# A linear-attention stage in four pipeline stages with row tiles of two heads, and softmax probabilities scaled before their transposes

## The reference, cut to what matters

```python
# block 1: linear attention, 16 heads of 16 features, chunks (64 in the reference; the kernel uses 128)
q = (q @ fq1.T + b) * (q @ fq2.T + b);  k = (k @ fk1.T + b) * (k @ fk2.T + b)
s = where(tril, qc @ kc.T, 0);  o = s @ vc + qc @ state;  state += kc.T @ vc
o = o * rsqrt(mean(o*o) + eps) * norm_w;  x = x + layernorm(o @ wo.T)
# block 2: softmax attention, 32 query heads in 8 groups of 4, head size 64, causal
attn = softmax(where(causal, q @ k.T / 8, min));  h = r + (attn @ v) @ wo
# then a mixture of 8 experts (top 2), then x = x + layernorm(h + moe)
```

## Time and profile before

| | us |
|---|---|
| median of three runs | 1934.72 |
| the profiled execution, its own time | 1933.22 |
| its span, first to last instruction | 1931.3 |
| PE busy in it | 1813.6 |
| DVE busy in it | 1055.0 |
| ACT busy in it | 924.1 |

### The profile page before, as it was taken

How to read it: one execution, slowest core, us unless ns; L and a number is a source line. 1 busy time by engine, 2 the same in 40 slices (tenths; PEclk the granted TensorE clock), 3 DMA queues, 4 the chain that set the end, 5 groups by cost and what they waited for, 6 DMA issues and landing times.

```text
span 1931.3 us, 32217 instructions
## 1 busy us (share of the span) xinstructions
PE 1813.6 (94%) x12286; PEld 1428.7 (74%) x12286; DVE 1055.0 (55%) x2465; ACT 924.1 (48%) x2049; POOL 261.1 (14%) x355
## 2 busy tenths in 40 slices
PE   6999689999999999999999999999985999999994
PEld 5666457777777777777777777777765999999993
DVE  3666556766776766767767667667655111111112
ACT  3343255655656656656656656656651222222223
POOL 2222110000000000000000000000001222222222
PEclk9999889999999999999999999999986999999997
DMA  2000010000000000000000000000017134213443
GB/s 83 0 0 0 0 44 1 9 1 1 9 1 1 9 1 1 10 1 1 9 1 1 9 1 1 1 1 1 23 34 245 22 92 128 48 26 87 119 125 95
DMA packets 46042, 60.02 MB, mean 31 GB/s; under 512 B 8944, under 2 KB 39536, under 8 KB 45936
## 3 DMA queue, kind: packets, MB, share of 16 engines
q1 hardware_dynamic: 36336, 46.16, 7.2%
q0 software_dynamic: 7536, 10.36, 3.2%
q10 hardware_dynamic: 2064, 2.10, 0.3%
HBM read 138.43 MB, written 11.40 MB: 78 GB/s over the span
## 4 chain that ended last, share of the span: by engine, by line
PE 86%; DVE 7%; ACT 2%; issue 2%; POOL 1%; DMA 1%; SPq 0%; DVEq 0%; POOLq 0%; ACTq 0%
PE wide L1401 15%; PE bank L1313 13%; PE bank L1301 12%; PE bank L1253 9%; PE wide L1285 8%; PE bank L1410 7%; PE wide L1286 7%; PE bank L1322 6%; PE wide L1120 2%; PE bank L1109 2%; PE bank L1298 1%; ACT qhl L634 1%; PE bank L1177 1%; DVE arena L802 1%; PE bank L1243 1%
## 5 line engine op out<-in xcount | busy, mean ns | idle before, releaser
L884 DVE CUSTOM_DVE_ANT_0 arena<-wide,arena 128x896 f32<-128x896 f32 (+7 forms) x512 | 383.8, 755 | 223.2 <-PE wide L1286 219.3
L640 ACT ACTIVATE arena<-arena,nmax 128x896 f32<-128x896 f32 (+7 forms) x512 | 397.0, 776 | 177.3 <-DVE nmax L884 174.2
L1285 PE MATMUL wide<-khi,qhl 128*128 128x512 f32 (+3 forms) x768 | 346.3, 452 | 1.7 <-DVE qhl L877 1.7
L1301 PE MATMUL bank<-ident,arena 128*128 128x128 f32 x2304 | 308.5, 274 | 0.0
L648 ACT COPY arena<-bank 128x512 f32<-128x512 f32 (+1 forms) x352 | 191.7, 545 | 214.0 <-PE bank L1301 206.3
L1401 PEld LDWEIGHTS wide<-wo,arena 128*128 128x128 f32 x2496 | 287.0, 193 | 3.2 <-issue 1.3
L1401 PE MATMUL wide<-wo,arena 128*128 128x128 f32 x2496 | 287.3, 277 | 0.9 <-ACT wo L693 0.9
L1313 PE MATMUL bank<-arena,vt 128*64 128x256 f32 x2304 | 277.0, 385 | 0.0
L1301 PEld LDWEIGHTS bank<-ident,arena 128*128 128x128 f32 x2304 | 262.3, 141 | 16.6 <-issue 0.4
L1286 PE MATMUL wide<-klo,qhl 128*128 128x512 f32 (+3 forms) x768 | 256.0, 347 | 0.0
L1050 DVE TENSOR_TENSOR wo<-wide,wo 128x512 f32<-128x512 f32 x78 | 53.9, 692 | 368.1 <-PE wide L1401 368.1
(11 more groups left out here) (221 smaller groups left out, 1749.8 us busy)
## 6 DMA issues: line engine op xcount, KB each, us to landing
arena<-in_L_ffn_w SPq DMA_DIRECT2D x117, 1024.0 KB
x_all<-in_L_attn_x ACTq DMA_DIRECT2D x1, 2048.0 KB, 9.9
wq_g<-in_L_ffn_wq SPq DMA_DIRECT2D x8, 256.0 KB, 3.5
wo<-in_L_ffn_wo SPq DMA_DIRECT2D x16, 128.0 KB, 3.0
hbuf<-acc SPq DMA_DIRECT2D x2, 1024.0 KB, 4.6
tbuf<-rT_all SPq DMA_DIRECT2D x4, 512.0 KB, 3.0
acc<-hbuf SPq DMA_DIRECT2D x4, 512.0 KB, 5.5
out<-x_all SPq DMA_DIRECT2D x8, 256.0 KB, 2.1
```

The lines of the kernel that those rows point to most:

```text
L640: nc.scalar.activation(probs[t % 2][:, h, 0:w], probs[t % 2][:, h, 0:w], ACT.Exp, bias=nmax[:, t % 2, h:h + 1], scale=-1.0, accum_out=rsum ...
L884: nc.vector.tensor_tensor_reduce(out=probs[t % 2][:, h, 0:w], in0=score_bank(t, h)[:, 0:w], in1=causal[:, SEQ - w:SEQ], scale=-1.0, scalar ...
L1285: mm(dst, q, khi[:, lo:lo + cols], start=True, stop=False)
L1301: ins = nc.tensor.transpose(to[:, h * P:(h + 1) * P], probs[t % 2][:, h, m * P:(m + 1) * P], ident[:])
```

## The change: what it does

In the linear-attention stage all loops are unrolled, and a tile goes through four steps where it went through two: front in step s, output in step s+1, layer norms in step s+2, last transpose in step s+3 (so there are 11 steps, of which 8 have a front). `qx` keeps two masked copies per half, with a mask that leaves one head of each 32 rows (`rowmask`); a score call is now 8 matmuls of 32 rows by 256 columns each, four row groups writing to four banks. There are two score calls per step, of 8 matmuls each. Masks 2 and 3 of a tile move to the next step. x is normalised by ScalarE (a new `xnmr`), the state add and the first residual add move from VectorE to GpSimd, and ScalarE copies the output projection to SBUF (`aos`).

In the softmax stage the spread block of `rinv` is gone from GpSimd and TensorE. VectorE multiplies each head's probabilities in place by the inverse row sum (`normalise`) and transposes wait for that. All block evacuations and the copy of the weighted values (`oT`) are ScalarE's.

```diff
-NCONST = 27
+NCONST = 29
+ROWS = 4
+HR = HB // ROWS
-    blocks = t % TB + 2
+    blocks = t % TB + 1
...
 # GpSimd, linear attention
-                    for b in range(BATCH):
-                        nc.gpsimd.tensor_tensor(qx[:, 0, b], qT[:, 0, b:b + 1, :].to_broadcast([P, HB, P]), ...
+                if back:
+                    power(s - 2, BATCH, rstds["ao"], ves["ao"], "ve_ao", "rstd_ao")
+                    gp.wait_ge(S("aon_ready"), s - 1)
+                    nc.gpsimd.tensor_tensor(xb, xb, aon, ALU.add).then_inc(S("x1_ready"), 1)
+                if mid and s < TB:
+                    nc.gpsimd.tensor_tensor(state, state, kvt, ALU.add).then_inc(S("state_ready"), 1)
+                if front:
+                    nc.gpsimd.tensor_tensor(qx[:, 0].rearrange("p b h c -> p h b c"), ... [P, HR, BATCH, P]), ALU.mult)
...
 # ScalarE, linear attention
-                    for h in range(HB):
-                        ins = nc.scalar.activation(qx[:, 1, :, h], qT[:, 1], ACT.Copy, scale=headmask[:, h:h + 1])
+                    for h in range(HR):
+                        ins = nc.scalar.activation(qx[:, 1, :, h], qT[:, 1], ACT.Copy, scale=rowmask[:, h:h + 1])
+                    nc.scalar.copy(aos, bank[0][:].rearrange("p (b d) -> p b d", b=BATCH)).then_inc(S("aos_ready"), 1)
+                if s + 1 < TB:
+                    normal_x(s + 1)
...
 # VectorE, linear attention: the order of a step
+                if mid:
+                    mask(s - 1, 2)
+                    mask(s - 1, 3)
+                if back:       # layer norm of aos, tile s-2
+                    variance(i, aos, "ao")
...            # q, then variance of x1, both reciprocals, k, onT, y
+                if front:
+                    mask(s, 0)
+                    mask(s, 1)
...
 # TensorE, linear attention
-                    for j in range(2):
-                        ins = mm(wide[:, 2 * b + j, :], kT[:, k, b], qx[:, k, b, j * 4:(j + 1) * 4]...)
+                def score(k):
+                    if s or k:
+                        pe.wait_ge(S("sm_ready"), 4 * s + 2 * k)
+                    for b in range(BATCH):
+                        for j in range(ROWS):
+                            rows = slice(j * P // ROWS, (j + 1) * P // ROWS)
+                            ins = mm(wide[:, j, b * HR * P:(b + 1) * HR * P], kT[rows, k, b], qx[rows, k, b]...)
...            # order: output(0), turn xn, turn rn (tile s-3), feature 0, output(1), feature 1, mean square,
...            # features 2 and 3, v, turn k, score(0), output projection, kv, score(1)
+            for s in range(TB + 3):
+                pair_step(s, s < TB, 1 <= s <= TB, s >= 3)
...
 # ScalarE, softmax
+                if weighing:
+                    act.wait_ge(S("o2_psum"), t - 1)
+                    nc.scalar.copy(oT[:], bank[2][:, 0:2 * P]...).then_inc(S("oT_ready"), 1)
-                    if j % 2 == 0:
+                    nc.scalar.copy(pT[t % 2][m], bank_of((t, m))).then_inc(S("pT_ready"), 1)
...
 # VectorE, softmax
+            def normalise(t, h):
+                if h % 2 == 0:
+                    invert(t, h // 2)
+                    v.wait_ge(S("rinv_ready"), 2 * t + h // 2 + 1)
+                nc.vector.tensor_scalar(probs[t % 2][:, h, 0:w], probs[t % 2][:, h, 0:w], rinv[:, t % 2, h:h + 1], None, ALU.mult)
...            # a row: maximum(t,0), normalise(t-1,2), (t-1,3), low_part, maximum(t,1), (t,2), normalise(t,0),
...            # add to acc (t-2), maximum(t,3), normalise(t,1)
 # TensorE, softmax
-                        pe.wait_ge(S("exp_done"), G * (t + 1))
-                    if m == t % TB + 1:
-                        pe.wait_ge(S("rinv_spread"), t + 1)
-                        for x in range(2):
-                            ins = nc.tensor.transpose(to[:, x * P:(x + 1) * P], spread[t % 2][:, x], ident[:])
+                        pe.wait_ge(S("probs_ready"), G * (t + 1))
```

More of the change, by code:

```diff
@@ L488, in _ @@
             double(0, 0)
[L489 to L501, removed]
+            for n in range(NSEQ):
+                for half in range(2):
+                    if n or half:
+                        double(n, half)
             gp.wait_ge(S("k_doubled"), 2 * NSEQ)
@@ L659, in _ @@
                     exponent(t, 0)
+                if weighing:
+                    act.wait_ge(S("o2_psum"), t - 1)
+                    nc.scalar.copy(oT[:], bank[2][:, 0:2 * P].rearrange("p (j c) -> p j c", j=2)).then_inc(S("oT_ready"), 1)
                 if turning:
@@ L801, in pair_step @@
                 if back:
-                    nc.vector.reciprocal(halves[0][:, 1], halves[1][:, 1]).then_inc(S("orstd_ready"), 1)
-                    v.wait_ge(S("orstd_ready"), s)
-                    nc.vector.tensor_tensor(whole(onT), bank[2][:], orstd[:], ALU.mult).then_inc(S("onT_ready"), 1)
+                    v.wait_ge(S("x1_ready"), i)
+                    variance(i, xb, "x1")
+                if mid:
+                    v.wait_ge(S("oms_ready"), s)
+                    for k in range(KB):
+                        ins = nc.vector.reciprocal(halves[0][:, k], halves[1][:, k])
+                    ins.then_inc(S("orstd_ready"), 1)
                 if front:
@@ L1170, in pair_step @@
                     feature(bank[1], 3, "k2_psum")
-                if back:
+                    if mid:
+                        pe.wait_ge(S("oms_ready"), s)
+                    for b in range(BATCH):
+                        for k in range(KB):
+                            ins = mm(bank[3][:, b * D:(b + 1) * D], xnT[:, k, b], wvT[:, k], start=(k == 0), stop=(k == KB - 1))
+                    ins.then_inc(S("v_psum"), 1)
+                    pe.wait_ge(S("kT_ready"), s + 1)
+                    turn(bank[1], lambda k, b: kT[:, k, b], "ktok_psum")
+                    score(0)
+                if mid:
                     pe.wait_ge(S("onT_ready"), s)
@@ L1200, in pair_step @@
                     ins.then_inc(S("kv_psum"), 1)
-                    score(3)
-                if back:
-                    pe.wait_ge(S("r_ready"), s)
-                    if front:
-                        pe.wait_ge(S("ktok_ready"), s + 1)
-                    turn(bank[1], lambda k, b: rn[:, b, k * P:(k + 1) * P], "rT_psum")
-            pair_step(0, True, False)
-            with pe.Fori(1, TB) as s:
-                pair_step(s, True, True)
-            pair_step(TB, False, True)
+                    score(1)
+            for s in range(TB + 3):
+                pair_step(s, s < TB, 1 <= s <= TB, s >= 3)
             pe.wait_ge(S("rT_ready"), TB)
```

329 lines of the change are left out of this document (148 added, 181 removed).

## The result

The kernel after takes 1849.19 us (median of four runs, 1847.24 to 1850.91), the kernel before in the same comparison 1934.07 us: ratio 0.9561, 95% interval 0.9547 to 0.9575. A second comparison gave 0.9562 (0.9548 to 0.9575).

The account below looks back on a forecast made before the run. VectorE and TensorE were to bound the changed linear-attention step, TensorE the softmax stage before the change. Linear attention -36 and softmax -10 gave 1933.2 - 46 = 1887, with the median 1.5 above: 1889 us, range 1853 to 1928.

Parts of the forecast that it names:

- the balance of the softmax stage: Softmax stage: 1.9 us of new stalls against 2.5 removed, so 0.6 us less per sequence, -10 us in all.
- the removals: Softmax stage: spread transposes (1.8 us) and the `oT` wait (0.7) leave TensorE's path, at most 2.5 us per sequence.
- the new stalls: Softmax rows of ct 3, 4, 7 and 0: TensorE waits 0.4, 0.9, 0.45 and 0.15 us, 1.9 per sequence.
- Scores: Linear-attention score matmuls: row groups cut 6.9 us per step to 2.6, saving 4.3.
- rival A: Linear-attention scores: row groups don't overlap, cost stays 6.9 us, step 24.3, kernel 1919 us; chance 0.12.
- Step: Linear-attention loop: a step takes 20.0 us against 25.66, bound by VectorE and TensorE together; 39.6 us less over 7 steps.
- Drain: End of the linear-attention stage, after the last score: 29.5 us for 25.6, 4 us more.
- Stage 1: Linear-attention stage: -39.6 + 4 = -36 us, bounds -43 and -6.
- the walk: Softmax rows: added engine work laid against each row's length, giving 1.9 us of stalls per sequence.
- Rival C: Both stages: no new softmax stalls and four-way row-group overlap, -43 - 39, 1853 us; chance 0.12.
- B: Softmax stage: ScalarE becomes the bound, exponents behind copies; 2.5 us more per sequence, +40, 1929 us; chance 0.09.
- D: Softmax scaling: one column at a time, VectorE 9.6 us more per sequence, TensorE sees 6; +96, 1985 us; chance 0.05.

## Why the prediction was wrong

The direction and both places were right. The step that failed is the balance of the softmax stage, "Sum 1.9 against 2.5: 0.6 us less per sequence, -10 us", and both of its terms were mis-sized: the removals gave about 3.3 us per sequence and not "at most 2.5", and the new stalls took about 0.6 and not 1.9. The stage gave 43.9 us, more than the 39 that the prediction called the most that could go.

- **Scores.** Forecast 2.6 us per step between 1.7 and 3.9; measured 2 x 1.08 = 2.16. With 3.46 a call on full rows, rival A's 6.9 was right for its own case. The pull toward a load-bound 3.9 cost 0.4 us per step. The Trainium skill, TensorE: Matmul & The Clock Gate, gives in "Part 3: Packing small matmuls" 3.07 times for 512 columns, and the runs show 3.2 for 256. The Trainium skill's rule in "LDWEIGHTS (loading the stationary operand)" of that page, a load's time by the columns of the weights, agrees with the single loads here (184 ns for 32 rows, 192 for 128). What failed is the reading that the loads follow one another: by it 3.0 us would be saved per step, and 4.7 were.
- **Step.** Forecast 20.0, measured 19.6. That is the score term. The prediction had VectorE and TensorE bind the step together; in the trace TensorE is busy for 19.36 of 19.60 us, and its score calls wait 1.5 us for the masks in the whole stage.
- **Drain.** Forecast 29.5 us, measured from the same point 205.83 - 177.75 = 28.1, so 2.5 us more than before and not 4. The output projection again ran at the low clock, 3.78 us (3.73 in the earlier trace rows). Stage 1 in all: -40.0 for -36.
- **What left the softmax path: the first half of the failed step.** Forecast 1.8 us for the spread block (8 x 0.22) and 0.7 for `oT`. From the table of rows the block and the wait for a bank behind it took 2.5 us, `oT` 0.7, and the item itself some 0.1 less behind it: 3.3. The one row of ct 5 that was read stood for eight. Nor are the two terms independent: without the move of `oT`, 7.8 us come back as its wait.
- **The new stalls: the other half.** Forecast 1.9 us per sequence: 0.4 in the row of ct 3, 0.9 in ct 4, 0.45 in ct 7, 0.15 in ct 0. Measured as what a row gave less than its share of the removals, they are 0.2 in ct 3 (0.31 less 0.12), 0.2 in ct 4 (0.22 less 0.04), 0.1 each in ct 7 and ct 1 and nothing in ct 0: 0.6. So 3.3 - 0.6 = 2.7 us per sequence, 43.9 us in the stage. Of the 34 us of error there, some 13 are the removals' and 21 the stalls'.
- **Why the stalls were oversized.** Three inputs of the walk were off. The windows read for the rows of ct 3 and ct 4, 6.0 and 9.0 us, begin 0.6 us late; the rows are 6.50 and 8.50 long, so the row of ct 3 had 0.5 us more room than the walk gave it, and the row of ct 4 0.5 less. The scalings were taken at 18.2 us per sequence and VectorE is busy with them for 16.1; of the 2.1 between, 1.4 are in their size (32 scalings of 525 ns by the mean, 16.8), as the fixed part is smaller. And the walk laid whole durations end to end. ScalarE's and VectorE's timelines of the kernel after, in the row of ct 7:

```profile
770.35 1.56 ACT L662 COPY arena<-bank 128x512 f32<-128x512 f32 x3
```

```profile
768.59 0.75 DVE L894 TENSOR_SCALAR arena<-arena,rinv 128x1024 f32<-128x1024 f32 x1
769.26 0.42 DVE L922 TENSOR_TENSOR acc<-bank,acc 128x256 f32<-128x256 f32 x1
```

  Three block copies of 586 ns take 1.56 us, so they start (1.56 - 0.586) / 2 = 0.49 apart; the scaling is 0.75 long, and what follows it starts after 0.67. For a sequence the forecast had VectorE at 53.3 and ScalarE at 56.8 us; they came to 51.2 and 53.9. The run with one more scaling puts VectorE at 54.2 and loses 1.6 + 0.6 = 2.2 us per sequence, near the forecast's 1.9. So the walk described a kernel with some 2 to 3 us more work in a sequence; a few tenths per row decided between 30 us of stalls and 9. How the 21 us divide among the three inputs is not measured.

Rival C (no new stalls and full overlap, 1853) came nearest. It was priced from the bounds, 39 us for softmax and 43 for stage 1; measured were 43.9 and 40.0. So its total is near for a reason that is partly luck: some stalls did appear, and the removals were larger than its bound. The range ended at C's time, and its end was too high by the part of the removals that was left out. What rivals B and D would have cost is now known in part: 7.0 us more on ScalarE cost 1.4 per sequence, 6.2 more on VectorE 2.15, where D had 6 of 9.6.

## What to carry to other kernels

Before a cost goes into a sum times the number of rows, read it in every kind of row: the spread block took 0.22 us in one and 0.51 in another, and the difference was a wait that only the weight loads show. Walk a tight schedule with distances from one start to the next, taken from a back-to-back group, and with row bounds taken from the same instruction; a stall that comes out at a few tenths then has a chance of its own and belongs in the range, not in the sum. When a run confirms a sum, check its terms too: 40 for 39 hid a wait of 9.3 us and removals some 13 us larger than forecast. Size the move of an operation off a loaded engine by the wait it would have after the rest of the change, not by the one it has before: `oT` was worth 11 us by its old wait and 26 in place. And row groups paid only in an order that had emptied all the banks they write: the same matmuls lost 10 us in the old one.

## What the runs showed of the hardware

- Float32 matmuls of 32 rows by 256 columns in four row groups start 0.067 us apart, on full rows 0.216: 3.2 times. Their weight loads last 184 ns each and still 16 of them take 0.74 us.
- In the old order a TensorE idle for 4.15 us came back at a granted clock of 0.50, and its next 16 records took 2.09 us for 1.15.
- VectorE's in-place scaling in SBUF takes 0.52 ns per column from 256 columns on (351 to 751 ns), but 128 columns take as long as 256 by the mean (347 ns).
- Neither VectorE at 54 of 72 us nor ScalarE at 61 of 72 is "busy", and both already cost TensorE 1.4 us or more per sequence: here the share said little of the slack.
